# Flamingo block on one core: x, context and x2 turned by DMA in f16 instead of on TensorE, and q and k laid out in scratch memory by head, part and channel

## The reference

```python
q = X @ Wq.T + bq; k = ctx @ Wk.T + bk; v = ctx @ Wv.T + bv      # X = layernorm(x)
scores = einsum('bgrqd,bgkd->bgrqk', q, k) / sqrt(16)            # 32 heads of 16 in 8 groups
scores = where(mask, -inf, scores); w = softmax(scores)
x = x + tanh(g_xattn) * (einsum('bgrqk,bgkd->bgrqd', w, v) @ Wo.T + bo)
x = x + tanh(g_ffn) * ((silu(h @ Wg * gs) * (h @ Wu * us)) @ Wd * ds)   # h = layernorm(x), F = 1536, fp8 weights
```

## Time and profile before

| | |
|---|---|
| runs | 617.63, 619.19, 616.64 us; median 617.63 |
| profiled execution | 622.37 us, its span 620.6 us |
| mean granted TensorE clock | 0.961 |
| busy, share of the span | PE 93%, DVE 80%, ACT 58%, PEld 58%, POOL 38% |
| chain that ended last | PE 79%, DVE 8%, DMA 3%, ACT 3% |
| DMA | 50.24 MB, mean 81 GB/s |

### The profile page before, as it was taken

The page is one execution under the profiler, slowest core; times in us unless marked ns, Lnnn a source line. Parts: engine busy times, 40 slices in busy tenths (PEclk is TensorE's granted clock), DMA queues, the critical chain, the costliest instruction groups (busy, mean ns, idle before and its releaser), DMA issues.

```text
span 620.6 us, 14382 instructions
## 1 busy us (share of the span) xinstructions
PE 574.9 (93%) x5165; PEld 359.2 (58%) x5165; DVE 497.2 (80%) x1527; ACT 362.4 (58%) x672; POOL 237.1 (38%) x323
## 2 busy tenths in 40 slices
PE   4686896699999999999999999999998999899997
PEld 4553362256754776467745775477644764476683
DVE  3687578989997999999999998998998898744321
ACT  4442666767764576466756675567733774475261
POOL 3200212100671158312753157215731365157184
PEclk9977899789999999999999999999998999799999
DMA  8594452772031312332131403013111020200000
GB/s 290 181 293 107 123 170 50 231 178 78 5 98 34 85 46 74 84 104 70 26 100 49 124 3 88 20 48 91 30 44 61 2 67 7 86 4 20 0 36 34
DMA packets 53872, 50.24 MB, mean 81 GB/s; under 512 B 7501, under 2 KB 41386, under 8 KB 53802
## 3 DMA queue, kind: packets, MB, share of 16 engines
q1 hardware_dynamic: 53280, 48.72, 27.5%
q10 hardware_dynamic: 522, 0.61, 0.3%
HBM read 35.15 MB, written 9.44 MB: 72 GB/s over the span
## 4 chain that ended last, share of the span: by engine, by line
PE 79%; DVE 8%; DMA 3%; issue 3%; ACT 3%; SPq 2%; POOL 0%; ACTq 0%; POOLq 0%; DVEq 0%
PE work L1186 26%; PE work L1197 12%; PE av L1086 9%; PE work L1164 7%; PE work L1117 6%; PE sc L1076 5%; PE sc L1058 5%; DVE junk L902 2%; PE work L1147 2%; DVE ws L911 2%; PE sc L1072 1%; PE work L1126 1%; PE work L1137 1%; PE work L1173 1%; DMA cin<-in_ctx 1%
## 5 line engine op out<-in xcount | busy, mean ns | idle before, releaser
L902 DVE CUSTOM_DVE_ANT_0 junk<-sc,mq 128x256 bf16<-128x256 f32 x496 | 179.9, 418 | 32.0 <-PE sc L1058 31.3
L911 DVE SCALAR_TENSOR_TENSOR ws<-sc,padc,mask_k 128x1024 f32<-128x1024 f32 x112 | 143.3, 1279 | 11.0 <-PE sc L1076 9.8
L768 ACT ACTIVATE ws<-ws 128x1024 f32<-128x1024 f32 x112 | 116.4, 1051 | 12.3 <-DVE ws L911 12.3
L697 POOL TENSOR_TENSOR ff<-ga,up 128x256 f32<-128x256 f32 x96 | 69.8, 732 | 137.0 <-DVE ga L992 135.8
L1186 PE MATMUL work<-h_h,wg 128*128 128x256 f16 x384 | 90.0, 275 | 0.0
L1186 PE MATMUL work<-h_l,wg 128*128 128x256 f16 x384 | 89.3, 273 | 0.0
L1186 PE MATMUL work<-h_l,wu 128*128 128x256 f16 x384 | 89.1, 273 | 0.0
L1186 PE MATMUL work<-h_h,wu 128*128 128x256 f16 x384 | 89.0, 272 | 0.0
L826 ACT ACTIVATE up<-work,fuse_s 128x256 f32<-128x256 f32 x96 | 45.0, 469 | 65.3 <-PE work L1186 64.5
L704 POOL TENSOR_TENSOR f_l<-ff,f_h 128x256 f16<-128x256 f32 x96 | 64.2, 679 | 36.3 <-ACT f_h L834 36.1
L1197 PE MATMUL work<-wd,f_h 128*128 128x512 fp8e4 x192 | 72.9, 380 | 0.0
(11 more groups left out here) (130 smaller groups left out, 1035.3 us busy)
## 6 DMA issues: line engine op xcount, KB each, us to landing
qs<-q_scratch SPq DMA_DIRECT2D x96, 64.0 KB, 2.5
cin<-in_ctx SPq DMA_DIRECT2D x8, 512.0 KB, 4.6
xin<-in_x SPq DMA_DIRECT2D x8, 512.0 KB, 5.0
xb<-in_x SPq DMA_DIRECT2D x8, 512.0 KB, 4.0
att_u<-un SPq DMA_DIRECT2D x128, 32.0 KB, 2.0
out_x<-yt SPq DMA_DIRECT2D x16, 256.0 KB, 2.2
ks<-k_scratch SPq DMA_DIRECT2D x48, 64.0 KB, 2.6
q_scratch<-qh SPq DMA_DIRECT2D x16, 128.0 KB, 3.7
```

The lines of the kernel that those rows point to most:

```text
L697: pool.tensor_tensor(ff[:, n % RING, :], ga[:, n % RING, :], up[:, n % RING, :], ALU.mult).then_inc(ff_done, 1)
L768: act.activation(ws[:, unit, :, :], ws[:, unit, :, :], ACT.Exp, scale=1.0 / SSC).then_inc(exp_done, 1)
L902: last = dve.tensor_tensor_reduce((junk, junk_1)[maxima_banks(n, b)][:, j, :], sc[maxima_banks(n, b)][:, place(j)], mq[b % 2][:, t, :], 1. ...
L911: dve.scalar_tensor_tensor(out=ws[:, n % 4, :, :], in0=sc[1][:, :].rearrange("p (j l) -> p j l", j=HPG), scalar=padc[b % 2][:, kt:kt + 1], ...
```

## The change

TensorE transposes neither x, nor the context, nor x2. ACT rounds the untransposed rows (128 x 512, f32 in SBUF) to f16 (xr_h, cr_h, h2r_h), GpSimd subtracts for the low half (xr_l, cr_l, h2r_l), and SyncE issues a transposing DMA (dma_start_transpose, 128 x 512 f16, 128 KB, SBUF to SBUF) for each half: 12 per batch. layernorm is written in place, into xin and xb. The pieces n = 0, 1 are now halves of the rows, so the first product of each kind waits for all four transfers (x_in, c_in, h2_in). The loads of x, context and xb wait for the low half of what was there before.

q_scratch and k_scratch are laid out as head, part (3), channel, with q's high half and k's high half written twice. A q half is put by 6 transfers and got by 2 of 192 KB, k put by 3 and got by 2 of 192 KB; the high halves of q are put as soon as they are there. The context is no longer scaled by 4; the scale has moved into Wk and v's factor.

The tables are gone: each engine's list is written out as words for all eight batches, in an order of its own for each batch. TensorE's is shown in full; the others have the same form.

```diff
+PIECES = {"maxima": 16, "scores": 16, "exp": 16, "weighted": 8, "sums": 8, "gu": 12, "fuse": 12, "fsplit": 12, "xT": 2,
+          "cT": 2, "x2T": 2, "q": 2, "mrow": 2, "spread": 2, "split_att": 2, "out": 2, "down": 2, "down_a": 2, "down_b": 2,
+          "slab": 12, "put_q": 2, "get_q": 2, "rows": 2, "gather": 2, "store": 2, "add_y": 2}
+
+
+def order(words, setup=(), by_pe=0):
+
+
+    pieces, seen = [], {"scores": PIECES["scores"] * by_pe, "load_x": 1, "load_c": 1}
+    for word in words.split():
+        name, _, times = word.partition("*")
+        for _ in range(int(times or 1)):
+            k = seen.get(name, 0)
+            seen[name] = k + 1
+            if name == "setup":
+                pieces.append((name, setup[k], 0))
+            elif name in ("power_0", "power_1"):
+                pieces.append(("power", int(name[-1]), k))
+            else:
+                pieces.append((name, k % PIECES.get(name, 1), k // PIECES.get(name, 1)))
+    return pieces
+
+
+WEIGHTS = [n for n, name in enumerate(SETUP) if name[0] == "W"]
+PE_ORDER = order("""
+    setup*12 q k q v maxima*8 k mrow maxima q maxima v maxima q maxima scores maxima scores maxima scores maxima
+    weighted scores maxima scores mrow maxima scores weighted maxima scores weighted maxima scores q maxima scores
+    weighted maxima scores k scores maxima q maxima weighted scores maxima*2 scores weighted maxima mrow scores
+    maxima scores maxima scores maxima weighted scores maxima weighted scores v maxima scores maxima weighted scores
+    mrow scores spread scores spread weighted scores maxima scores maxima out*2 weighted maxima scores q maxima k
+    scores weighted maxima scores q scores weighted maxima scores gu maxima gu scores maxima weighted gu mrow maxima
+    scores gu maxima weighted scores gu maxima scores gu weighted maxima scores gu v maxima scores gu*3 scores
+    maxima weighted spread gu scores maxima down_a spread maxima scores gu weighted scores maxima out scores maxima
+    mrow out down_a weighted scores maxima q scores maxima down_b*2 maxima scores weighted k maxima scores q maxima
+    scores weighted gu scores maxima weighted gu mrow scores maxima gu weighted maxima scores gu maxima gu scores
+    maxima gu weighted scores maxima gu v maxima scores gu*2 maxima scores gu*2 weighted maxima scores spread*2 gu
+    weighted maxima scores down_a mrow scores maxima out maxima scores weighted out scores maxima k q down_b scores
+    maxima weighted down_a maxima scores weighted down_b scores maxima q scores maxima weighted gu mrow scores
+    maxima gu*2 maxima scores gu scores gu maxima scores weighted gu scores maxima weighted gu scores maxima gu*2
+    weighted scores maxima v gu spread gu scores maxima spread gu maxima weighted q scores maxima down_a maxima
+    scores out mrow out weighted scores maxima k down_a maxima scores down_b scores maxima weighted down_b maxima
+    scores q maxima scores gu weighted maxima scores gu maxima weighted scores gu maxima scores mrow gu*2 maxima
+    scores weighted gu maxima scores v weighted maxima scores gu scores gu*3 maxima scores spread gu weighted maxima
+    scores gu spread weighted scores maxima down_a maxima scores mrow out scores maxima out weighted scores maxima
+    down_a q maxima scores weighted down_b scores maxima down_b scores maxima q maxima scores weighted gu scores
+    maxima weighted gu scores maxima mrow gu*2 maxima scores gu maxima weighted k maxima scores gu scores gu maxima
+    scores weighted gu maxima scores gu*3 scores maxima weighted spread*2 gu weighted scores maxima down_a scores
+    maxima out maxima scores mrow out maxima down_a weighted maxima scores down_b scores weighted maxima scores
+    down_b maxima scores weighted v maxima scores gu weighted scores maxima gu*2 maxima scores mrow gu weighted
+    maxima scores gu maxima gu scores maxima weighted gu maxima scores gu*3 scores maxima weighted spread gu spread
+    scores gu maxima scores down_a weighted scores maxima out mrow scores out weighted scores down_a scores down_b
+    scores weighted scores down_b scores weighted scores gu scores gu weighted scores gu scores weighted gu weighted
+    gu*5 spread gu spread gu*2 out*2 down_a*2 down_b*2 gu*12 down_a*2 down_b*2
+""", range(len(SETUP)))
...
-        q_dram = nc.dram_tensor("q_scratch", [2, D, L], f16, kind="Internal").ap()
-        k_dram = nc.dram_tensor("k_scratch", [2, KV, L], f16, kind="Internal").ap()
+        q_dram = nc.dram_tensor("q_scratch", [H, 3, HD, L], f16, kind="Internal").ap()
+        k_dram = nc.dram_tensor("k_scratch", [G, 3, HD, L], f16, kind="Internal").ap()
...
                 if name == "load_x" and b:
-                    sp.wait_ge(normed[0], 2 * b)
+                    sp.wait_ge(x_low, 2 * b)
                     sp.dma_start(xin[:, :, :], x_v[b]).then_inc(ld_x, 16)
                 if name == "load_c" and b:
-                    wait_ready(sp, "cT", 1, b - 1)
+                    sp.wait_ge(c_low, 2 * b)
                     sp.dma_start(cin[:, :, :], c_v[b]).then_inc(ld_c, 16)
                 if name == "load_xb":
+                    past(sp, x2_low, 2 * b)
+                    sp.dma_start(xb[:, :, :], x_v[b]).then_inc(ld_xb, 16)
+                if name == "xT":
+                    sp.wait_ge(x_high, 2 * b + n + 1)
                     if b:
-                        wait_free(sp, "out", 1, b - 1)
-                    sp.dma_start(xb[:, :, :], x_v[b]).then_inc(ld_xb, 16)
+                        wait_ready(sp, "q", 1, b - 1)
+                    sp.dma_start_transpose(xh[:, :, n * P:(n + 1) * P], xr_h[:, n, :]).then_inc(x_in, 16)
+                    sp.wait_ge(x_low, 2 * b + n + 1)
+                    sp.dma_start_transpose(xl[:, :, n * P:(n + 1) * P], xr_l[:, n, :]).then_inc(x_in, 16)
+                if name == "x2T":
+                    sp.wait_ge(x2_high, 2 * b + n + 1)
+                    if b:
+                        wait_ready(sp, "gu", FT - 1, b - 1)
+                    sp.dma_start_transpose(h2_h[:, :, n * P:(n + 1) * P], h2r_h[:, n, :]).then_inc(h2_in, 16)
+                    sp.wait_ge(x2_low, 2 * b + n + 1)
+                    sp.dma_start_transpose(h2_l[:, :, n * P:(n + 1) * P], h2r_l[:, n, :]).then_inc(h2_in, 16)
+                if name == "cT":
+                    sp.wait_ge(c_high, 2 * b + n + 1)
+                    if b:
+                        wait_ready(sp, "v", 0, b - 1)
+                    sp.dma_start_transpose(ch[:, :, n * P:(n + 1) * P], cr_h[:, n, :]).then_inc(c_in, 16)
+                    sp.wait_ge(c_low, 2 * b + n + 1)
+                    sp.dma_start_transpose(cl[:, :, n * P:(n + 1) * P], cr_l[:, n, :]).then_inc(c_in, 16)
                 if name == "put_q":
-                    wait_free(sp, "q", n, b)
-                    past(sp, qs_in[n], 96 * b)
-                    for part, src in enumerate((qh, ql)):
-                        sp.dma_start(q_dram[part, 2 * n * P:2 * (n + 1) * P, :].rearrange("(t p) n -> p t n", p=P),
-                                     src[:, 2 * n:2 * n + 2, :]).then_inc(q_out[n], 16)
+                    sp.wait_ge(q_high, 2 * b + n + 1)
+                    past(sp, qs_in[n], 32 * b)
+                    for s, src in ((0, qh), (2, qh), (1, ql)):
+                        if s == 1:
+                            wait_free(sp, "q", n, b)
+                        for t in (2 * n, 2 * n + 1):
+                            sp.dma_start(q_dram[8 * t:8 * t + 8, s, :, :], src[:, t, :]).then_inc(q_out[n], 16)
                 if name == "get_q":
-                    sp.wait_ge(q_out[n], 32 * (b + 1))
+                    sp.wait_ge(q_out[n], 96 * (b + 1))
                     past(sp, t_ready, 16 * (b - 1))
                     for hf in range(2):
-                        for s in range(3):
-                            src = q_dram[(0, 1, 0)[s], 2 * n * P:2 * (n + 1) * P, :]
-                            sp.dma_start(qs[b % 2][64 * hf + HD * s:64 * hf + HD * (s + 1), 8 * n:8 * n + 8, :],
-                                         src.rearrange("(p f d) n -> f d p n", f=2, d=HD)[hf]).then_inc(qs_in[n], 16)
+                        src = q_dram[16 * n:16 * (n + 1), :, :, :].rearrange("(p f) s d n -> f (s d) p n", f=2)[hf]
+                        sp.dma_start(qs[b % 2][64 * hf:64 * hf + 3 * HD, 8 * n:8 * n + 8, :], src).then_inc(qs_in[n], 16)
                 if name == "put_k":
                     wait_free(sp, "k", 0, b)
-                    past(sp, ks_in, 96 * b)
-                    for part, src in enumerate((kh, kl)):
-                        sp.dma_start(k_dram[part], src[:, :]).then_inc(k_out, 16)
+                    past(sp, ks_in, 32 * b)
+                    for s, src in enumerate((kh, kh, kl)):
+                        sp.dma_start(k_dram[:, s, :, :], src[:, :]).then_inc(k_out, 16)
                 if name == "get_k":
-                    sp.wait_ge(k_out, 32 * (b + 1))
+                    sp.wait_ge(k_out, 48 * (b + 1))
```

(64 more changed lines are left out.)

401 lines of the change are left out of this document (90 added, 311 removed).

## The result

The changed kernel takes 635.05 us (median, 631.24 to 636.19) beside 618.41 for the kernel before: a ratio of 1.0248, 95% interval 1.0191 to 1.0305. It is slower by 2.5%, where the forecast was 598 us and faster; the stated range, 584 to 636 us, holds it by 1 us. The profiled execution has a span of 629.4 us (before 620.6).

The account below looks back on a forecast made before the run. TensorE was taken to bound the kernel from 140 to 540 us, VectorE close behind. Steady part -17.5, x2 +4, end 0, start -3 and -3 sum to -19.5 us, against 617.63: 598 us, range 584 to 636.

Parts of the forecast that it names:

- What leaves TensorE: TensorE, per batch: 24 transposes go, 2.91 us; six pitches fall from 66.9 to 64.0 us, -17.5 us in all.
- The sum of 598: Whole kernel: -17.5 + 4 + 0 - 3 - 3 = -19.5 us, set against the median 617.63: 598 us.
- The queue's sum: SyncE's queue, per batch: 32.6 us plus 12 transposing issues of 0.8, so 42 of 64 us.
- It becomes the bound at 2.6 us each: SyncE's queue: transposing issues make it the bound only from (64.0 - 32.6) / 12 = 2.6 us per transfer.
- q and k stand 24 to 66 us before their first maxima: Batches 3 to 7: this distance hides x's and the context's four transfers of 0.8 us plus a 3.8 us landing.
- x2's chain: From out product to gate-up: 14.7 us against TensorE's cover, short by 2.4 and 1.9 in batches 0 and 6: +4 us.
- Rival (b): x2 chain outgrows its cover: issues of 2.1, landings of 7.3, 5.8 us idle per batch, 640 us; chance 0.20.
- The start: Up to the first maxima (38.48 before, 34 after) -3 us, and from there to 140 us another -3.
- The end: Last batch: x2's 11.7 us against 10.4 of cover; before, 9.2 plus a half product, 11.9 together; equal, 0.
- The added puts: SyncE's queue, per batch: 15 puts (+4.2) and 6 gets (-5.5), 1.3 us net, counted as nothing in the steady part.
- The rule against it: Skill advises TensorE (390 ns against DMA's 1309): by it 5.2 us per transfer, kernel near 810 us; not used in the sum.
- The chances: Whole kernel: faster 0.69, same 0.06, slower 0.25; the forecast's own range, 590 to 606 us, had 0.50.

Follow-up runs that it names:

- plain copies: Changed kernel with each of the 96 transposing transfers replaced by a plain copy of the same 128 KB, operands not turned: 599.89 us, ratio 0.9688.
- plain copies, old layout: Changed kernel with plain copies for the transposing transfers (operands not turned) and the old scratch layout back: 598.01 us, ratio 0.9703.
- merged, old layout: Changed kernel with high and low half turned by one 128x1024 transfer, 6 per batch, and the old scratch layout: 602.44 us, ratio 0.9736.
- merged: Changed kernel with high and low half of a row tile turned by one 128x1024 transfer, 6 transposing issues per batch for 12: 609.29 us, ratio 0.9850.
- plain copies in two: Plain-copy kernel with each 128 KB copy split into two of 64 partitions, 24 issues per batch, operands not turned: 630.83 us, ratio 1.0221.
- transposes, old layout: Changed kernel with the old scratch layout back (q and k put and got as before), DMA transposes and orders kept: 626.71 us, ratio 1.0121.
- transposes in two: Changed kernel with each transposing transfer split by columns into two of 128x256: 737.91 us in its one execution.

## Why the prediction was wrong, point by point

**What leaves TensorE: right in kind, too small.** I had 8 x 2.9 = 23 us. With plain copies, where TensorE hardly waits, its busy time is 546.2 us, 28.7 less than before. The changed kernel shows 21.5 less: the same 4973 matmuls take it 553.4 us, at a granted clock of 0.98 in the middle where plain copies have 1.00, and these 7 us are a part of the loss beside the waits. VectorE's and GpSimd's terms were near (28.1 for 32.8; 7.0 us per batch on GpSimd, 53.5 / 8 = 6.7 measured).

**The sum of 598: met by plain copies, in part by luck.** They take 599.89 us. But by the marks the first comes 3.3 us late where I had 6 early, the six batches after it gain 26.2 where I had 17.5 (less some 2 for x2), and the stretch behind the last loses 1.1. Of the 26.2 only 7.2 come in the four middle batches (64.8 us each in place of 66.6); 11.1 and 7.9 come in the first and the last of the six. The new orders may have moved work across these marks; my sum did not price that, and no run takes it apart.

**The queue's sum: an undersized term.** I took 0.8 us for a transposing issue; it is 1.26. I took 0.47 for a put; in the new layout it is 0.57. Together that adds 12 x 0.46 + 15 x 0.10 = 7 us per batch, 49 where I had 42 of 64. The trace has 47.1 of 69.0 us per batch in the middle (issues alone); a gather's hold is 0.65 there and not 0.73, since I had divided a row that has small gaps in it. Both new values lay in my bounds (0.37 to 2.1), and below the 2.6 from which I said it would decide.

**"It becomes the bound at 2.6 us each": the step that failed.** I compared the queue's load with the length of a batch, and took everything as hidden below that: what stands behind a transpose in the queue would "wait 2 us at most", with readers "further away than that". The load table shows how wrong that is. Its second column is the sum of SyncE's single issues over the whole trace, without the gaps between them; the last is the same per batch, between the out marks of batches 1 and 5, and the length of a batch there.

| kernel (all with the new orders) | SyncE's issues, us | span, us | issues of a batch's length, us |
|---|---|---|---|
| plain copies, old layout | 322.7 | 596.2 | 38.8 of 64.6 |
| plain copies | 331.2 | 598.7 | 39.2 of 64.8 |
| merged, old layout | 333.7 | 602.1 | 40.4 of 64.6 |
| merged | 346.9 | 606.0 | 40.8 of 65.6 |
| plain copies in two | 390.6 | 630.7 | 46.5 of 69.0 |
| transposes, old layout | 394.9 | 624.5 | 47.1 of 68.0 |
| changed kernel | 399.7 | 629.4 | 47.1 of 69.0 |
| transposes in two | 515.9 | 736.1 | 62.3 of 81.0 |

At 39 to 41 us per batch, about what I had put the queue at, TensorE is all but full in the middle (394 to 398 of 400 us); at 47 (385 to 388), with 22 us of the batch free in the queue, it no longer is. Over the whole table another us of issues costs about 0.4 of one up to the changed kernel and 0.9 beyond. Between 347 and 391 us there is no kernel, so where the loss sets in isn't shown, and the kernels differ in more than this sum: a pattern, not a law. The queue is "full" long before its sum is, since its work comes in bursts. This one stands before TensorE's longest wait after 140 us in the changed kernel, by the timelines of SyncE, GpSimd and TensorE:

```profile
429.33 1.21 SPq L467 DMA_TRANSPOSE ch<-cr_h  x1
...
431.96 2.54 SPq L477 DMA_DIRECT2D q_scratch<-qh  x4
...
435.81 1.20 SPq L467 DMA_TRANSPOSE ch<-cr_h  x1
437.06 1.26 SPq L469 DMA_TRANSPOSE cl<-cr_l  x1
438.43 2.40 SPq L477 DMA_DIRECT2D q_scratch<-qh  x4
440.88 1.17 SPq L477 DMA_DIRECT2D q_scratch<-ql  x2
...
442.60 1.42 SPq L502 DMA_DIRECT2D qs<-nm_h  x2
444.07 1.30 SPq L502 DMA_DIRECT2D qs<-nm_l  x2
...
434.81 0.66 POOL L587 TENSOR_TENSOR nm_l<-nm,nm_h 16x256 f16<-16x256 f32 x1
...
446.54 0.61 PE L939 MATMUL sc<-qs,ks 50*128 50x256 f16 x4 [5.14 <-DMA qs<-nm_l]
```

GpSimd has the maxima's low row ready at 435.5 us. SyncE, at work without a gap of over 0.2 us since 429.33, comes to it at 444.07, and TensorE stands still for 5.14 us. With plain copies the same row is ready at 414.2 and issued at 417.66, 3.4 us later and not 8.6.

What the late transfers cost is in TensorE's waits in the changed kernel (us in total, times, longest):

```profile
PE sc L939 <- DMA qs<-nm_l: 9.7, 4, 5.1
...
PE work L980 <- DMA cl<-cr_l: 7.2, 2, 4.8
...
PE sc L921 <- DMA qs<-q_scratch: 4.4, 1, 4.4
...
PE work L1019 <- DMA h_l<-h2r_l: 3.3, 3, 1.6
...
PE work L970 <- DMA xl<-xr_l: 1.8, 2, 1.3
```

They come to 26.4 us. With plain copies the first two are 1.0 and 0.5 and the other three are not there. With the 7 us of longer busy time this is the 30.7 us between the two spans, to within 2. The largest of them, the maxima's rows, I had put at nothing: they are not turned at all, they stand behind transfers that are, and behind the puts.

**"q and k stand 24 to 66 us before their first maxima": the wrong cover.** That distance is from q to whoever reads q. But q itself has a fixed place in TensorE's list, and an in-order engine stands still there if x is late, however long before the maxima that is. The cover of a transfer ends where its reader stands in the list of that reader's engine, and I measured it to the reader's reader. In the batches of that sentence this cost little. A case where x is late, by SyncE's and TensorE's timelines:

```profile
256.77 1.04 SPq L483 DMA_DIRECT2D qs<-q_scratch  x2
...
272.57 1.23 SPq L453 DMA_TRANSPOSE xh<-xr_h  x1
273.84 1.26 SPq L455 DMA_TRANSPOSE xl<-xr_l  x1
...
278.36 0.28 PE L970 MATMUL work<-xh,wq_h 128*128 128x256 f16 x1 [1.27 <-DMA xl<-xr_l]
```

x's low halves were ready at 251.0 and 252.8 (ends of GpSimd's rows), and the last is issued at 273.84, 21 us later: from 256.77 to 275.10 the queue is never idle for over half a microsecond. TensorE comes to q at 277.1 and gets x at 278.36. So 21 us of lateness cost 1.27 us here, and all waits for x 1.8. The context's 7.2 us are from batches 0 and 2, before 140 us.

**x2's chain: the size by luck, and not the cause.** I gave it +4 us, in batches 0 and 6; TensorE's waits for h_l come to 3.3, and they stand in batches 2, 5 and 7, with none in 0 and 6. Rival (b) thus came near the time (640) by another mechanism than its own: not one chain that outgrows its cover but a queue in which each of several transfers is late. The landings of 7.3 us did not come; x2's were 2.5 (median).

**The start: wrong by 21 us.** I had -6 up to batch 0's out product and measured +15. 11.7 of it go with plain copies, so they are the queue; the other 9 are errors of mine. Three rows of TensorE, the first from the kernel before, the others from the changed one:

```profile
31.34 0.61 PE L1058 MATMUL sc<-ks,qs 48*128 48x256 f16 x4 [4.60 <-DMA qs<-q_scratch]
...
42.04 1.04 PE L921 MATMUL sc<-ks,qs 48*128 48x256 f16 x8 [7.60 <-DVE wo_l L751]
...
59.33 0.61 PE L921 MATMUL sc<-ks,qs 48*128 48x256 f16 x4 [4.40 <-DMA qs<-q_scratch]
```

The kernel before has its first maxima at 31.34 us. The 38.48 that I took for them is a later maxima piece, which the chain shows because it stands behind the context's transposes; so even my own 34 meant 3 us later and not 4.5 earlier. The change has them at 42.04, and their last wait is for VectorE's wo_l, a piece of the set-up, not for a transfer; it is there with plain copies too (until 40.23). The next pieces wait 4.40 us for a get of q that stands behind eight transposes in the queue (42.51 to 53.53).

**The end: the chain right, its price not.** From out's mark at 581.41 to the gate-up it is 11.9 us where I had 11.7:

```profile
590.82 2.48 DMA h_l<-h2r_l
...
593.35 21.13 PE work L1019 x192
```

But before it was 9.2, and the half product that the new order took from ahead of out gave nothing back there: from batch 6's mark to batch 7's it is 45.43 us (before 45.55). So I had 0, and it is 2.7 of the 2.9 us lost behind the last mark.

**The added puts: right alone, wrong in company.** "I give this edit nothing in the steady part" holds in the kernel before (1.0008) and with plain copies (0.9703 and 0.9688). With transposes it costs 1.3 points, and 1.1 with merged ones. The issues do not explain that: they differ by 5 us in all with transposes (8 us of time), by 13 with merged ones (4 to 7 us) and by 9 with plain copies (2 us). The get of 192 KB lands later (3.8 to 4.4 us in place of 2.5 to 2.8), but with plain copies too, where it costs nothing that can be told. Why the new layout costs time where transposes stand in the queue stays open.

**The rule against it.** The Trainium skill (VectorE: DVE Perf Modes, Rules for kernel authors) advises TensorE where PSUM will do. That agrees with the change as it was made (1.0248) and not with merged transposes by DMA (0.9850 and 0.9736, with the new orders in it). What I worked out from its other section, The three transpose paths, failed: x2's transfers of 128x512 land 2.5 us after their issue and an issue holds the queue for 1.26, so the four blocks are not four times 1.3 us one after another. And I had held a pace against its 390 ns: 0.11 to 0.13 us is how fast transposes follow one another on TensorE here, while one of them takes 302 to 318 ns in this trace (mean, f32). What spoke against the DMA was the issue's hold, of which that section says nothing.

**The chances.** 0.25 for slower was too little. The unknown issue time was worth 35 us between 0.53 (a plain copy's) and 1.26, inside the bounds that I had drawn and far from the threshold that I had set, and I let it decide nothing. Of my signs of being wrong two came, a batch over 67 us (69.0) and a granted clock below 1.00 in the middle (0.98); the one on the issue, above 2.6 us, did not.

## What to carry to other kernels

Before moving work from an engine to a DMA queue, add up how long each issue holds the queue, and do not take an in-order queue as hidden until it is full: here 41 of 65 us did no harm and 47 of 69 did. Ask of everything that stands in the queue, not only of what is new, what is ahead of it when its data are ready. A transfer's cover ends at its reader's place in the list of the reader's engine. Here a transposing issue's hold did not depend on its size, so merge such transfers before anything else: one of 1024 columns for two of 512 turned a loss of 2.5% into a gain of 1.5%, with the old layout of 2.6%. Test an issue's price by splitting and by plain copies; and do not give DMAs to a compute engine because it has idle time, since each holds up whatever stands behind it there (0.6 us each on ACT here).

## What the runs showed of the hardware that was not expected

A transposing issue from SyncE holds its queue for 1.24 us with 256 columns, 1.26 with 512 and 1.27 with 1024 (medians), while x2's transfers land 2.4, 2.4 to 2.5 and 3.1 us after it (medians). The Trainium skill (DMA: Bandwidth & Descriptors, Rules for kernel authors) says to coalesce small transfers; these runs agree, though for the queue's sake, well above the size that it names, 64 KB. A put of 64 KB whose rows go to eight heads in scratch memory holds the queue for 0.57 us, one of 128 KB by channel 0.41 to 0.47. ACT is held by its own issues as long as SyncE is: 0.585 us each (median of q's 64 puts).
